# A three-stage kernel on one core: first gate block in halves, one normalisation on ScalarE, bisection steps moved, the edges of the expert stage reordered

## Time and profile before

| what | value |
|---|---|
| median of the runs | 2772.85 us |
| profiled execution, its span | 2772.81 us, 2771.1 us |
| PE busy | 2714.9 us (98%) |
| VectorE, ScalarE, GpSimd busy | 1854.2, 1369.4, 696.5 us |
| mean granted TensorE clock | 0.997 |
| PE busy, 198.2 to 900 us | 701.8 of 701.8 us |
| PE busy, 1337 to 2755.4 us | 1418.2 of 1418.4 us |
| DMA issue to landing, x in 1 MB (gate) | 8.8 us median, 5.2 the first |
| DMA issue to landing, x in 256 KB (mixer) | 2.8 us median |

### The profile page before, as it was taken

The page is one execution under the profiler, slowest core; times in us unless marked ns, Lnnn a source line. Parts: engine busy times, 40 slices in busy tenths (PEclk is TensorE's granted clock), DMA queues, the critical chain, the costliest instruction groups (busy, mean ns, idle before and its releaser), DMA issues.

```text
span 2771.1 us, 40477 instructions
## 1 busy us (share of the span) xinstructions
PE 2714.9 (98%) x12168; PEld 2199.4 (79%) x12170; DVE 1854.2 (67%) x3098; ACT 1369.4 (49%) x2317; POOL 696.5 (25%) x1009
## 2 busy tenths in 40 slices
PE   7899999999999999999999999999999999999997
PEld 3578888888888877777788888888888888888886
DVE  8768888888877888888754555455554555455554
ACT  4644555555555566564544444444444444444443
POOL 4422222222222212124322122122222122122221
PEclk9999999999999999999999999999999999999999
DMA  9733223223333333336133042331422314314221
GB/s 348 251 122 106 89 88 97 96 93 95 95 98 99 107 107 107 107 90 208 64 92 83 18 123 55 76 87 23 119 66 50 103 32 107 78 25 121 40 46 16
DMA packets 118953, 265.11 MB, mean 96 GB/s; under 512 B 23968, under 2 KB 24160, under 8 KB 114784
## 3 DMA queue, kind: packets, MB, share of 16 engines
q1 hardware_dynamic: 84512, 164.83, 17.8%
q0 software_dynamic: 34240, 97.85, 15.2%
HBM read 208.86 MB, written 53.77 MB: 95 GB/s over the span
## 4 chain that ended last, share of the span: by engine, by line
PE 87%; DVE 6%; ACT 3%; issue 2%; DMA 1%; POOL 0%; DVEq 0%; ACTq 0%; POOLq 0%
PE po L1892 8%; PE po L1894 8%; PE po L1893 8%; PE ring L1479 8%; PE ring L1480 8%; PE ring L1481 8%; PE pb L1892 4%; PE pc L1892 4%; PE pb L1894 4%; PE pc L1894 4%; PE pb L1893 4%; PE pc L1893 4%; PE po L1517 3%; PE po L1518 3%; PE po L1519 3%
## 5 line engine op out<-in xcount | busy, mean ns | idle before, releaser
L1479 PE MATMUL ring<-xt_h,w_h 128*128 128x512 f32 x1024 | 400.7, 391 | 3.5 <-DVE xt_l L500 2.6
L1892 PE MATMUL po<-w2h,hid_h 128*128 128x512 f32 x1024 | 398.7, 389 | 1.1 <-DVE hid_l L1853 1.1
L1480 PE MATMUL ring<-xt_l,w_h 128*128 128x512 f32 x1024 | 398.8, 389 | 0.0
L1894 PE MATMUL po<-w2h,hid_l 128*128 128x512 f32 x1024 | 398.6, 389 | 0.0
L1481 PE MATMUL ring<-xt_h,w_l 128*128 128x512 f32 x1024 | 398.4, 389 | 0.0
L1893 PE MATMUL po<-w2l,hid_h 128*128 128x512 f32 x1024 | 398.4, 389 | 0.0
L1281 DVE SCALAR_TENSOR_TENSOR u<-xin,cw,u 128x512 f32<-128x512 f32 x384 | 288.4, 751 | 59.0 <-issue 29.7
L1820 ACT ACTIVATE hid<-pb,b1c 128x512 f32<-128x512 f32 x128 | 88.3, 690 | 395.9 <-PE pb L1894 391.6
L1743 POOL DMA_INDIRECT out_dram<-res,idx_c x64 | 101.0, 1578 | 721.8 <-DVE res L1879 662.3
L1853 DVE TENSOR_TENSOR hid_l<-hid,hid_h 128x512 fp32r<-128x512 f32 x128 | 88.7, 693 | 266.1 <-ACT hid_h L1824 255.0
L1853 DVE TENSOR_TENSOR hid_l<-xn_tail,hid_h 128x512 fp32r<-128x512 f32 x128 | 88.5, 692 | 231.4 <-ACT hid_h L1824 223.5
(11 more groups left out here) (214 smaller groups left out, 5952.0 us busy)
## 6 DMA issues: line engine op xcount, KB each, us to landing
wo<-wo_halves POOLq DMA_DIRECT2D x120, 512.0 KB, 4.0
w1r<-fc_in SPq DMA_DIRECT2D x130, 256.0 KB, 2.7
w2r<-fc_in SPq DMA_DIRECT2D x130, 256.0 KB, 2.9
g_x<-x_in SPq DMA_DIRECT2D x16, 1024.0 KB, 8.8
x_tail<-x_in SPq DMA_DIRECT2D x64, 256.0 KB, 2.8
out_dram<-res SPq DMA_DIRECT2D x64, 256.0 KB, 2.2
xt_rows<-g_xnt SPq DMA_DIRECT2D x15, 1024.0 KB, 10.6
rows<-xt_rows SPq DMA_DIRECT2D x15, 1024.0 KB, 6.9
```

What stands on the lines that cost most here:

```text
L1479: pe.matmul(ring[r % 2][:, :], w_h[:, r, q], xt_h[:, k, :], start=(k == 0), stop=False)
L1480: pe.matmul(ring[r % 2][:, :], w_h[:, r, q], xt_l[:, k, :], start=False, stop=False)
L1892: pe.matmul(dst, ah, bh, start=start, stop=False)
L1894: return pe.matmul(dst, al, bh, start=False, stop=stop)
```

## The change

**Gate.** The first block is loaded by two DMAs of two row tiles each. VectorE does its statistics per half, GpSimd the root per half (`first_half`), and PE transposes the first half when it is normalised. In every other block VectorE normalises three row tiles and ScalarE the fourth, one block ahead, between its weight copy and its score copy. The gate values of block 14 go behind xt_l.

**Mixer.** In block 0 the first two bisection steps go to between u_l(7) and the scan; their tallies follow share_b(6) and share_b(7); the third has its count at c = 1, its tally at c = 2 and its halve at c = 4. In block 15 ScalarE takes gate tile 7 before y_high(2), and no longer makes the row sums; VectorE's fc2 low part of tile 0 goes behind the last xt_l.

**Experts.** In the first group the row sums are made by ScalarE at s = 0 to 3, `add_beta` and `inverse_std` by GpSimd behind the gathers of group 1; ScalarE loads the GELU table ahead by an activation of one column. PE waits for the fc2 parts in front of the share, not of hidden. Turn 0 (on GpSimd and ScalarE) and turn 7 (on all four) are written out. The last group has no gathers, statistics, transposes or weight halves for a next one; the prefetch of two weight tiles, the padding of b1 and of the list go. Its last three shares go by row tile (`END_SHARES`), after hidden(15).

```diff
@@ gate: sync, gpsimd
-        load_x(0, 0)
+        sp.dma_start(xt[0][:, 0:HALF, :], x_v[at(0)][:, 0:HALF, :]).then_inc(c_first, 16)
+        sp.dma_start(xt[0][:, HALF:J, :], x_v[at(0)][:, HALF:J, :]).then_inc(c_x[0], 16)
+        def first_half():
+            h = slice(0, HALF)
+            pool.wait_ge(c_mv, HALF + 1)
+            pool.sem_inc(p_tick, 1)
+            pool.tensor_scalar(std[:, h], mv[0][:, h, 1], EPS, None, ALU.add).then_inc(c_eps, 1)
+            pool.wait_ge(c_eps, 1 + 1)
+            pool.tensor_tensor(rstd[0][:, h], std[:, h], half[:, h], ALU.pow).then_inc(c_eps, 1)
...
+            if type(b) is not int or b >= 3:
+                pool.wait_ge(c_xa, b - 2 + 1)
@@ gate: vector
+        def first_statistics():
+            for r, loaded in ((range(HALF), c_first), (range(HALF, J), c_x[0])):
+                dve.wait_ge(loaded, 16 + 1)
+                for j in r:
+                    dve.bn_stats(stats[:, j, :], xt[0][:, j, :]).then_inc(c_bn, 1)
+                dve.wait_ge(c_bn, r[-1] + 1 + 1)
+                for j in r:
+                    dve.bn_aggr(mv[0][:, j, :], stats[:, j, :]).then_inc(c_mv, 1)
...
         def normalise(b, i):
             dve.wait_ge(c_rs, b + 1 + 1)
-            for j in range(J):
+            for j in range(ON_DVE):
...
-                if not (first and i == 0):
+                if not (first and i == 0 or last and i == R - 1):
                     gate_values(dve, b - 1)
...
             dve.tensor_tensor(ew.yt_l[0][:, k, :], pt[k][:, :], f(ew.yt_h[0][:, k, :]),
                               ALU.subtract).then_inc(c_tl, 1)
+        gate_values(dve, NB - 2)
@@ gate: scalar
+        def normalise(b, i):
+            act.wait_ge(c_nb, 4 * b + 2 + 1)
+            for j in range(ON_DVE, J):
+                act.activation(xt[i][:, j, :], xt[i][:, j, :], ACT.Identity, bias=shift[i % 2][:, j:j + 1],
+                               scale=rstd[i % 2][:, j:j + 1]).then_inc(c_xa, 1)
...
                 if not (last and i == R - 1):
                     w_high(b, h, i)
+                    normalise(b + 1, (i + 1) % R)
@@ mixer: scalar
             side(1)
+            if last:
+                in_g(b, 7)
             y_high(b, 2)
...
                 ends.normal_rows(act, b, k)
-                if last and k >= 1:
-                    ends.sum_rows(act, b, k - 1)
             if last:
                 group_high(KD - 1)
-                ends.sum_rows(act, b, J - 1)
@@ mixer: vector
         def bisect_0(c):
-            if c in (3, 5, 7):
-                halve(c // 2 - 1, pb)
-            if c in (1, 3, 5):
-                count(c // 2)
+            if c == GAP:
+                count(0)
+                halve(0, pc)
+                count(1)
+                halve(1, pc)
+            if c == 1:
+                count(2)
+            if c == 4:
+                halve(2, pb)
@@ mixer: tensor
         def bisect_0(c):
-            if c in (1, 3, 5):
-                tally(c // 2, pb)
+            if c == GAP:
+                tally(0, pc)
+            if c == GAP_2:
+                pe.wait_ge(c_gain, 1 + 1)
+                tally(1, pc)
+            if c == 2:
+                tally(2, pb)
...
             share_b(b, 6)
+            side(GAP)
             in_step(b, 10)
             share_b(b, 7)
+            side(GAP_2)
@@ experts: gpsimd
-        for j in range(J):
-            ends.add_beta(pool, NB - 1, j)
-        ends.inverse_std(pool, NB - 1)
-        with pool.Fori(0, E) as e:
+        def pair(e, first=False, last=False):
             for i in range(2):
                 g = 2 * e + i
-                gather(g + 1, 1 - i)
-                ew.inverse_std(pool, g + 1, ends.half)
-                gather_gates(g + 1, 1 - i)
+                if not (last and i == 1):
+                    gather(g + 1, 1 - i)
+                    if first and i == 0:
+                        for j in range(J):
+                            ends.add_beta(pool, NB - 1, j)
+                        ends.inverse_std(pool, NB - 1)
+                    ew.inverse_std(pool, g + 1, ends.half)
+                    gather_gates(g + 1, 1 - i)
                 scatter(g, i)
@@ experts: vector
     def first_low(dve, s):
-        if s == 1:
+        if s == 0:
+            w_low(dve, 0, 0, (0,))
+        else:
+            w_low(dve, 0, 0, (1,))
             dve.wait_ge(c_bias, 16 + 1)
             bias(dve, 0, 0, 0)
-        w_low(dve, s, s)
+            w_low(dve, 1, 1)
@@ experts: scalar
-        act.wait_ge(ends.c_po, (NB - 1) * J + 1 + 1)
-        with act.Fori(0, E) as e:
+        act.activation(warm[:, :], ends.half[:, 0:1], ACT.Gelu_apprx_tanh)
+        def pair(e, first=False, last=False):
...
+                    if first and i == 0 and s == 1:
+                        act.wait_ge(ends.c_po, (NB - 1) * J + 1 + 1)
...
-                    next_high(e, i, s)
-                    if s - 1 in T_AT:
+                    if not (end and s + 2 >= FT):
+                        next_high(e, i, s)
+                    if first and i == 0 and s < J:
+                        ends.sum_rows(act, NB - 1, s)
+                    if s - 1 in T_AT and not end:
                         t_high(g + 1, T_AT.index(s - 1), 1 - i)
@@ experts: tensor
         def hidden(g, s, i):
             n = g * FT + s
-            pe.wait_ge(c_wl, 2 * n + 2 + 1)
+            pe.wait_ge(c_wl, 2 * n + 1 + 1)
...
+    END_SHARES = ((0, A), (0, B), (1, A), (0, C_), (1, B), (1, C_), (2, A), (2, B), (2, C_), (3, A), (3, B), (3, C_))
...
+                if last and i == 1:
+                    for s in range(1, FT - 3):
+                        hidden(g, s, i)
+                        out_share(g, s - 1)
+                    hidden(g, FT - 3, i)
+                    hidden(g, FT - 2, i)
+                    out_share(g, FT - 4)
+                    hidden(g, FT - 1, i)
+                    end_shares(g)
+                    continue
```

More of the change, by code:

```diff
@@ L406, in gpsimd @@
                            base=0, pattern=[[-1, P]], channel_multiplier=1).then_inc(c_id, 1)
+        def first_half():
[5 more added lines that the diff above has]
+            pool.tensor_tensor(rstd[0][:, h], std[:, h], half[:, h], ALU.pow).then_inc(c_eps, 1)
         def turn(b, i):
             here = bass.ds(at(b) * J, J)
+            first = type(b) is int and b == 0
+            h = slice(HALF, J) if first else slice(0, J)
+            if first:
+                first_half()
             pool.wait_ge(c_mv, (b + 1) * J + 1)
@@ L1227, in turn @@
                 w_high(4)
-            in_g(b, 7)
+            if not last:
+                in_g(b, 7)
             side(2)
@@ L1682, in stage_experts @@
     c_bias = m.count("f_bias")
-    c_pad = m.count("f_pad")
     c_b1 = m.count("f_b1")
@@ L1709, in sync @@
                 ew.load(sp, e + 1, i)
-        for i in range(2):
-            sp.wait_ge(c_wl, 2 * ((G - 1) * FT + i + 1) + 1)
-            ew.load(sp, 0, i)
     def gpsimd(pool):
@@ L1845, in tail, with pair @@
                 ends.finish(dve, NB - 1, s - 2)
-        def pair(e, first=False):
+        def pair(e, first=False, last=False):
             for i in range(2):
                 g = 2 * e + i
+                end = last and i == 1
                 for s in range(FT):
@@ L1936, in last_shares, with end_shares, pair @@
                 share(j, FT - 1)
+        def end_shares(g):
+            ready = FT - 3
+            for j, s in END_SHARES:
+                if s >= ready:
+                    pe.wait_ge(c_wl, 2 * (g * FT + s + 1) + 1)
+                    pe.wait_ge(c_hl, g * FT + s + 1 + 1)
+                    ready = s + 1
+                share(j, s)
         pe.wait_ge(sums.c_tl, (NB + 1) * KD + 1)
-        with pe.Fori(0, E) as e:
+        def pair(e, last=False):
             for i in range(2):
@@ L1950, in tensor @@
                 last_shares(g)
+        with pe.Fori(0, E - 1) as e:
+            pair(e)
+        pair(E - 1, last=True)
     return sync, gpsimd, vector, tensor, scalar
```

102 lines of the change are left out of this document (71 added, 31 removed).

## The result

The changed kernel takes 2755.83 us (median of four runs, 2755.53 to 2756.93); the kernel before, beside it, 2773.05. The ratio is 0.9937 (95% interval 0.992 to 0.9955): 17.2 us less, against a forecast of 2758.0. The profiled execution took 2755.53 with a span of 2753.8 (before: 2771.1), so the two traces differ by 17.3 us, and these can be laid out between marks that both have.

A forecast was written before the change was run, and what follows sets the result against it. TensorE was taken to bound two stages but not their edges, so gains come only where it waits or loses work: gate 8.5, first mixer block 3.1, first expert group -0.1, last group 3.3; 2772.8-14.8 = 2758.0 us, range 2753 to 2764.

The forecast's parts named there:

- Gate, start: Gate's first blocks: loading in halves brings block 1's transposes from 21.22 to 18.2 us, 3.0 early.
- Gate, middle: Gate's blocks up to 12: shorter VectorE period and earlier start bring block 12's transposes to 85.0, 5.0 us early.
- floors: Earliest times for block 12's transposes in the gate: 83.2 us by compute, 86.4 if loads only keep today's pace.
- rival (a): Gate's middle is held by the transfers: gate gain 3.0 us less, 5.8 at most, time 2761; chance 0.22.
- Gate, end: Gate's last blocks: 1.0 us from block 12 to 15, 2.5 from gate values placed behind the last xt_l.
- First mixer block: Mixer block 0: stall 2.5 and half clock 1.6 go, tally costs 0.65, gate-tile wait 0.3; gain 3.1 us.
- Last block and first group: Mixer's end and first expert group: first share 2.8 us early, given back by a stall at hid_l(3); balance -0.1.
- rival (c): Clock falls after the first expert group's stall and still in the first mixer block: 1.6 us each, 2761.2; chance 0.13.
- Last group: Last expert group: dropped transposes 1.9 us, shares by row tile and earlier scatters 1.45; gain 3.3 in all.
- What follows the last scatter: Kernel's end, after the last scatter: unchanged, gain 0.
- (d): Faster gate loop crowds the transfers, rate sinks to 311 GB/s for the whole middle; time 2774.7, chance 0.05.

The follow-up runs named there:

- d1: Changed kernel plus eight unread unit-matrix products in TensorE's idle stretch ahead of the gate's second block; 2756.39 us.
- d2: Changed kernel with the edits of b1, b5 and d1 together; 2751.29 us, ratio 0.992 to the kernel before.
- b4: Changed kernel with a quarter of the bytes in twelve of the gate's sixteen input-weight loads; 2755.06 us.
- b6: Changed kernel with VectorE's first statistics held until both halves of the first x block have landed; 2756.55 us.
- b5: Changed kernel with the three loads of w_c (twice) and w_b issued ahead of the first x reloads; 2755.17 us.
- e1: Changed kernel with the gate values of the last but one block back ahead of VectorE's four low halves; 2759.41 us.
- a2: Kernel before with only block 0's new bisection order in the mixer; 2769.31 us.
- a1: Kernel before with the gate's edits alone; 2764.90 us.
- a3: Changed kernel with the gate and block 0 as before, leaving the last block, first expert group and last group changed; 2770.79 us.
- b2: Changed kernel with ScalarE's gate tile 7 of the last block back behind y_high(2); 2755.89 us.
- b1: Changed kernel with GpSimd's inverse deviation of the last block issued behind the second row tile's beta, not the fourth; 2752.97 us.
- c1: Changed kernel with the last twelve shares in the order of the kernel before; 2756.13 us.

## Why the prediction was right, step by step

The time came 2.2 us under the forecast, within its range, and the gains were in the named places. That it came so near is partly luck: the gate gave 0.9 less than its term, the first mixer block 2.3 more, and 0.95 behind the last scatter was not foreseen. The first two sizes have reasons that the runs show, in the main.

- **Gate, start** (3.0): block 1 came 2.44 early, not 3.0 (18.78 against 18.2). What failed is the step behind it: I carried the early start through the middle and did not ask what TensorE does between block 0 and a block 1 that VectorE can't make as early. It idles, and the clock falls: 1.56 us (7.30 instead of 5.74 from block 1 to block 2). d1 and d2 fill the stretch and it does not fall; in b4 and b6 the stretch is shorter and it does not either. Of the 3.0 there is 1.2 left at block 2 (26.08 against 27.26).
- **Gate, middle** (5.0; block 12 at 85.0 between floors of 83.2 and 86.4): block 12 came at 86.28, 3.7 early. Without the clock's fall it comes at 84.90 (d1), so the 1.3 missing are that step's, not this one's. Both floors were good: 83.58 in d2, where neither clock nor transfer is in the way, and x landing at 74.82, forecast at 75.0 if the loads keep today's pace. That rival (a) would be the bound is half right: the transfers hold one block, the twelfth in order, for about 1.0 us (b5), not the middle for 3.
- **Gate, end** (1.0 and 2.5): 1.24 from block 12 to 15, and 2.63 from there to the mixer. e1 gives 2.1 for the order alone.
- **First mixer block** (3.1): 5.4. The stall of 2.49 and the half clock of 1.6 went, as forecast; the tally costs 0.42, not 0.65. The step that failed is "a wait of about 1.0 for the seventh gate tile stays, maybe 0.2 longer": it went. Laid product against product, block 0 gains 1.25 us there, 3.4 at the stall and the tallies that stood near it, and 1.6 by the clock, and pays 1.16 at the two new tallies, of which 0.6 is the wait. So about 1.5 of the 2.3 by which the term was too small is this wait; the rest is small parts, among them that a stall costs more than its idle time, for which the term had nothing. The slowest of the eight stores of the output weights' halves, for which ScalarE's copy waits, takes 5.6 to 5.8 us in the three traces with the old bisection order and 3.9 to 4.2 in all eleven with the new one. That it is the order's doing is shown (a2 has it, a1 and a3 have not); by what way, is open, since the stores are issued at nearly the same distances.
- **Last block and first group** (-0.1): -0.55 at the first group's first scatter, and each piece was there. First share 2.5 early (2.8), the stalled step 2.3 longer (2.3), 0.8 in the four steps behind (0.6). What failed is a small step: that gate tile 7 ahead of y_high(2) wins and loses nothing; it costs 0.44 (b2), and without it the first share is 2.94 early. The 0.0 in the table is the luck of the long stretch behind. b1 shows that the cause of the stall was the one named. The clock, which rival (c) let fall here, did so in four of nine traces.
- **Last group** (3.3): 3.4, of another make: TensorE 1.4 (2.0 without the new order, by c1; the wait of 0.35 takes back 0.6), the scatters 1.97 (1.45). c1 gives 1.36 of these to the order; the other 0.6 is VectorE, which no longer makes weight halves for nobody before its first result.
- **What follows the last scatter** ("unchanged"): 0.95 less in the changed kernel. It is 11.5 to 11.8 us in the three traces with the old end (before, a1, a2) and 10.7 to 11.05 in the eleven with the new one, so it belongs to the edits of the expert stage; no run tells to which of them.

Of the rivals, (d) is out: transfers ran at 387 GB/s from 25 to 86 us, no slower than before, and at 358 from 60 to 75 us, where they were slowest. The Trainium skill ("HBM Reference", Specifications (TRN2)) puts a core that streams alone well above its share of 358 GB/s, at about 425. With that the trace agrees, with 387 over 61 us; the share by itself, which the prediction weighed, does not bind here.

## What to carry to other kernels

When an engine's first piece of work is pulled forward, look at what its second piece waits for: the hole between them can take back a good part of what the start gave, by the clock (here 1.56 of 2.44 us), and eight products that nobody reads were worth 1.1 to 1.4 us. Where work is moved from one stage into the next, go through the queue of the engine that it lands on and put what others wait for ahead of what only has to be done: one call moved up by two rows was worth 3.0 us. And look for an edit's worth at the nearest mark behind it: 0.4 us that showed at once were gone in the spread 1246 us later.

## What the runs showed of the hardware

- TensorE's granted clock fell to its lower level, 1.2 of 2.4 GHz, after idle stretches of 2.35, 2.37, 2.67, 2.69, 2.76, 2.86 and 3.07 us ahead of the gate's second block (seven traces; block 2 then comes 7.29 to 7.35 us after block 1), and not after 1.41, 1.59, 1.61 and 1.81 (four traces, 5.74 us). After 2.49 us in the first mixer block it fell in three traces of three (before, a1, a3). After one and the same stall of 2.1 us in the expert stage it fell in four traces of nine, and after the 2.6 us ahead of the mixer it fell in a2_block0 and not in the kernel before or a3_end. So at this length it is not the stall alone that decides, and a price for it is a chance times about 1.0 to 1.6 us.
- A wait cost TensorE more than the idle time that the profile gives it: 0.35 us at the last shares came to 0.6 (from one product's start to the next 0.73 instead of 0.23, and 0.1 behind), 0.98 for the seventh gate tile to 1.25, and 2.14 in the expert stage to 2.3 in its step.
- x of the gate's blocks is asked for behind the transposes of the block four before it, so a transfer-bound point moves with the compute that it seems to hold. Block 12's x landed at 73.43 and 73.65 where block 8's transposes came at 60.01 and 60.62 (d1, b6), and at 74.35 to 75.83 in the six traces in which they came at 61.10 to 61.53. Within these six it does not follow them; 1.5 us of spread are the transfers' own.
